# A recurrence whose dense small products are cut apart by large ones, with two additions moved from VectorE to GpSimd

## The reference

```python
q, k, v = x @ Wq, x @ Wk, x @ Wv          # 16 heads of 16
g = sigmoid(x @ Wf + bf)
def step(state, inp):                     # 128 tokens, one after the other
    qt, kt, vt, gt = inp
    state = state * gt[..., None] + vt[..., None] * kt[..., None, :]
    return state, einsum('bhij,bhj->bhi', state, qt)
```

## Time and profile before

| | us |
|---|---|
| median of 3 runs (2298.08 to 2299.51) | 2299.24 |
| the profiled execution: its own time | 2293.58 |
| its span, first to last instruction | 2291.9 |
| TensorE matmul busy | 2122.2 (93%) |
| TensorE weight load busy | 1440.3 (63%) |
| VectorE busy | 1663.3 (73%) |
| ScalarE busy | 1145.6 (50%) |
| GpSimd busy | 311.0 (14%) |

### The profile page before, as it was taken

One profiled execution on the slowest core, in us unless ns is written; L12 is line 12 of the kernel. 1 busy time (PEld: TensorE's weight loads), 2 busy tenths in 40 slices (PEclk: granted clock), 3 DMA queues, 4 the chain that ended last, 5 costly groups with the idle time before them and its releaser, 6 DMA issues. The chain is left out here.

```text
span 2291.9 us, 74706 instructions
## 1 busy us (share of the span) xinstructions
PE 2122.2 (93%) x30263; PEld 1440.3 (63%) x30263; DVE 1663.3 (73%) x3010; ACT 1145.6 (50%) x1887; POOL 311.0 (14%) x282
## 2 busy tenths in 40 slices
PE   6989998989989869999999999999899999999698
PEld 4666666666666657777777777776444444444487
DVE  7777776777777757677776767775555558989897
ACT  3444443444444436766667676665211118855365
POOL 5000000000000011111111111111000005445221
PEclk9999999999999979999999999999899999999899
DMA  3010010010000010101101010100000004459674
GB/s 107 21 30 22 25 27 21 23 29 21 26 26 21 21 47 30 42 27 34 35 27 41 27 41 27 41 27 1 1 0 0 0 1 192 192 211 424 233 269 163
DMA packets 78311, 146.48 MB, mean 64 GB/s; under 512 B 10035, under 2 KB 63542, under 8 KB 78134
## 3 DMA queue, kind: packets, MB, share of 16 engines
q1 hardware_dynamic: 78134, 143.70, 17.9%
HBM read 82.84 MB, written 60.82 MB: 63 GB/s over the span
## 5 line engine op out<-in xcount | busy, mean ns | idle before, releaser
L1281 PE MATMUL ff_bank<-ff_xq,w_uh 128*128 (+1 forms) x1536 | 457.8, 380 | 2.8 <-ACT ff_whole L1390 2.8
L1281 PE MATMUL ff_bank<-ff_xq,w_ul 128*128 (+1 forms) x768 | 291.5, 380 | 0.0
L1281 PEld LDWEIGHTS ff_bank<-ff_xq,w_uh 128*128 128x128 f16 x1536 | 149.9, 98 | 181.3 <-issue 4.1
L1595 DVE TENSOR_REDUCE ff_top<-ff_bank 128x512 f32 (+1 forms) x192 | 132.7, 691 | 116.7 <-PE ff_bank L1281 116.7
L465 ACT ACTIVATE x<-rec_e 128x512 f32<-128x512 f32 x192 | 112.0, 596 | 176.9 <-PE rec_e L348 176.9
L1390 ACT ACTIVATE ff_whole<-ff_bank,ff_coef 128x512 int16<-128x512 f32 x192 | 124.5, 682 | 103.5 <-PE ff_bank L1281 46.4
L1062 DVE TENSOR_REDUCE mneg<-att_s 128x4 f32<-128x512 f32 x256 | 158.9, 683 | 21.1 <-PE att_s L819 20.3
L600 DVE TENSOR_TENSOR rec_tmp<-rec_x,x 32x256 f32<-32x256 f32 (+1 forms) x192 | 80.8, 421 | 126.9 <-PE rec_x L385 62.1
L564 DVE TENSOR_TENSOR x<-rec_x,rec_until 128x512 f32<-128x512 f32 x256 | 158.4, 679 | 12.8 <-PE rec_x L332 12.0
L360 PE MATMUL rec_x<-x 32*32 32x64 f32 x8192 | 147.9, 218 | 21.3 <-issue 12.0
L360 PEld LDWEIGHTS rec_x<-x 32*32 32x32 f32 x8192 | 124.6, 106 | 59.3 <-issue 58.8
(11 more groups left out here) (236 smaller groups left out, 4406.9 us busy)
## 6 DMA issues: line engine op xcount, KB each, us to landing
gate_scratch<-ff_out SPq DMA_DIRECT2D x28, 768.0 KB, 3.5
ff_in<-gate_scratch SPq DMA_DIRECT2D x28, 768.0 KB, 11.0
product_scratch<-ff_out SPq DMA_DIRECT2D x28, 768.0 KB, 9.7
ff_out<-product_scratch SPq DMA_DIRECT2D x28, 768.0 KB, 5.9
att_x<-in_x SPq DMA_DIRECT2D x32, 256.0 KB, 2.7
att_ctx<-in_ctx SPq DMA_DIRECT2D x32, 256.0 KB, 2.9
att_o<-rec_scratch SPq DMA_DIRECT2D x32, 256.0 KB, 3.7
out<-s_out SPq DMA_DIRECT2D x16, 512.0 KB, 3.3
```

What stands on the lines that cost most here:

```text
L1281: m = T.matmul(bank_[:], weights(wp, kc, a, c), tile[:, xp, kc], start=(i == 0), stop=(i == len(terms) - 1))
L1595: V.tensor_reduce(top[:, k, bass.ds(n, 1)], banks[k % 6][:], AX.X, ALU.max, apply_absolute_value=True).then_inc(q1["maxed"], 1)
```

## The change

- **Exponents.** Five sums instead of seven (NE). One matmul result now gives several exponentials: `USES` lists, for each sum, which are taken, `DONE` how many are ready after it. ScalarE takes ten exponentials as before, eight of them with a per-lane bias (`hidden`) that hides the lanes for which they do not hold; before it was four of ten.
- **TensorE's order.** q goes between S0 and S1 in place of vg1. Q is cut in two halves of 32 products with vg0 of the next pair between them. The turn goes between e and I3. vg1 of the next pair comes last in the step. The order is: S0, q, S1, k, I0, k, I1, e, I2, e, turn, I3, e, H, Q first half, vg0, Q second half, e, e, vg1.
- **VectorE.** `floor` comes ahead of the scores, both `scores_out` follow each other, `weighted` part 0 moves to the step of its own pair, between `half_out` and `quarter_out`. L578 (nh) goes to ScalarE. L621 and L623 go to GpSimd (`gather`).
- **GpSimd.** `gather` for each pair; the eight weight-rounding instructions are put one by one behind the first eight gathers.
- The constants are smaller by one mask for each sequence.

```diff
-    NE = 3 + NR
-    EXPS = NR + NE - 1
+    NE = 5
+    EXPS = 2 * NR + 2
+    USES = (((0, 0), (0, 2), (1, 0), (1, 2)), ((0, 1), (1, 1)), ((0, 3), (1, 3)), ((0, NR),), ((0, NR + 1),))
+    DONE = (4, 6, 8, 9, 10)
...
+                def gather(n, s, before):
+                    out = o[:, s].rearrange("p (h i) -> p h i", i=HD)
+                    pool.wait_ge(stored[s], DMAS * (before + 1))
+                    pool.wait_ge(q["added"], 2 * n + 1)
+                    G.tensor_tensor(out, tmp[:, :, 0], tmp[:, :, 1], ALU.add).then_inc(q["added"], 1)
+                    pool.wait_ge(q["added"], 2 * n + 2)
+                    G.tensor_tensor(out, out, tmp[:, :, 2], ALU.add).then_inc(q["out_ready"], 1)
+
+                def levelled(n, flat, r, s, turn_):
+                    if n:
+                        c.wait()
+                    if turn_ in (0, 3):
+                        x = s if turn_ else r
+                        c.did(G.tensor_tensor(blocks_of(flat), blocks_of(flat), spread(x, flat), ALU.mult))
+                    else:
+                        c.did(G.tensor_scalar(flat, flat, 1.0, MAGIC if turn_ == 1 else -MAGIC, ALU.mult, ALU.add))
+
+                for n in range(8):
+                    gather(n, n % 2, n // 2)
+                    levelled(n, *((flat_u, ru, su), (flat_d, rd, sd))[n // 4], n % 4)
+                with pool.Fori(0, (NP - 8) // 2) as j:
+                    for u in range(2):
+                        gather(2 * j + 8 + u, u, j + 4)
...
-                def across_quarter(n):
-                    pe.wait_ge(q["o_taken"], TAKES * n + TAKES + 2)
-                    pe.sem_inc(q["seen"], 1)
-                    for hd in range(H):
+                def across_quarter(n, part):
+                    if part == 0:
+                        pe.wait_ge(q["o_taken"], TAKES * n + TAKES + 2)
+                        pe.sem_inc(q["seen"], 1)
+                    for hd in range(part * HH, (part + 1) * HH):
                         for b in range(2):
                             at = slice(b * D + hd * HD, b * D + (hd + 1) * HD)
                             for chunk in (0, 2):
                                 src, dst = rows(place(b, chunk)), rows(place(b, chunk + 1))
                                 m = T.matmul(X[1][dst, at], mt[src, b, hd, dst], wa[src, 0, at], start=True, stop=True)
-                    m.then_inc(q["o_made"], 1)
+                    if part == 1:
+                        m.then_inc(q["o_made"], 1)
...
                 def products(p, n, s, so, front, back):
                     if back:
                         scores(n, so, 0)
                     if front:
-                        value_gate(p, 1)
+                        across(p, 0, F[1], 0, 0, q["q_made"])
+                        across(p, 0, F[1], 0, 1, q["q_made"])
                     if back:
                         scores(n, so, 1)
                     if front:
-                        across(p, 0, F[1], 0, 0, q["q_made"])
-                        across(p, 0, F[1], 0, 1, q["q_made"])
                         across(p, 1, F[0], 1, 0, q["k_made"])
 
                 def pieces(p, s, before, front, back, more):
                     n, so = p - 1, 1 - s
-                    for i in range(8):
-                        if back:
-                            if i < 4:
-                                inside(n, so, i)
-                            elif i == 4:
-                                across_half(n)
-                            elif i == 5:
-                                across_quarter(n)
-                        if front and i == 0:
-                            across(p, 1, F[0], 1, 1, q["k_made"])
-                        if more and i == 4:
-                            turn(p + 1, so, before + s)
-                        if more and i == 7:
-                            value_gate(p + 1, 0)
-                        if front and i >= 1:
-                            exponents(p, s, i - 1)
+                    if back:
+                        inside(n, so, 0)
+                    if front:
+                        across(p, 1, F[0], 1, 1, q["k_made"])
+                    if back:
+                        inside(n, so, 1)
+                    if front:
+                        exponents(p, s, 0)
+                    if back:
+                        inside(n, so, 2)
+                    if front:
+                        exponents(p, s, 1)
+                    if more:
+                        turn(p + 1, so, before + s)
+                    if back:
+                        inside(n, so, 3)
+                    if front:
+                        exponents(p, s, 2)
+                    if back:
+                        across_half(n)
+                        across_quarter(n, 0)
+                    if more:
+                        value_gate(p + 1, 0)
+                    if back:
+                        across_quarter(n, 1)
+                    if front:
+                        exponents(p, s, 3)
+                        exponents(p, s, 4)
+                    if more:
+                        value_gate(p + 1, 1)
...
+                    act.wait_ge(q["lg_ready"], p + 1)
+                    A.activation(nh[:], nl[:], ACT.Copy).then_inc(q["h_ready"], 1)
...
-                    for k in range(NE - 1):
+                    for k in range(NE):
                         act.wait_ge(q["e_made"], NE * p + k + 1)
-                        A.activation(e[:, s, k], E[(s + k) % 2][:], ACT.Exp).then_inc(q["e_ready"], 1)
-                        if k == 2 and not (isinstance(p, int) and p == NP - 1):
+                        for asks, r in USES[k]:
+                            out = um[:, s, r] if asks else e[:, s, r]
+                            A.activation(out, E[(s + k) % 2][:], ACT.Exp, bias=hidden[:, asks, r:r + 1] if r < NR else 0.0,
+                                         scale=-1.0 if asks else 1.0).then_inc(q["e_ready"], 1)
+                        if k == 1 and not (isinstance(p, int) and p == NP - 1):
                             turned(p + 1)
-                    act.wait_ge(q["e_made"], NE * p + NE)
-                    for r in range(NR):
-                        A.activation(um[:, s, r], E[s][:], ACT.Exp, bias=hidden[:, r:r + 1]).then_inc(q["e_ready"], 1)
...
-                    V.tensor_copy(nh[:], nl[:]).then_inc(q["n_ready"], 1)
-                    dve.wait_ge(q["n_ready"], 2 * p + 1)
                     V.tensor_tensor(nlo[:], nl[:], nh[:], ALU.subtract).then_inc(q["n_ready"], 1)
...
-                def total(n, s, before):
+                def total(n):
                     dve.wait_ge(q["o_taken"], TAKES + TAKES * (n + 1))
                     V.tensor_tensor(tmp[:, :, 0:3], tmp[:, :, 0:3], tmp[:, :, 3:6], ALU.add).then_inc(q["added"], 1)
-                    out = o[:, s].rearrange("p (h i) -> p h i", i=HD)
-                    dve.wait_ge(stored[s], DMAS * (before + 1))
-                    dve.wait_ge(q["added"], 2 * n + 1)
-                    V.tensor_tensor(out, tmp[:, :, 0], tmp[:, :, 1], ALU.add).then_inc(q["added"], 1)
-                    dve.wait_ge(q["added"], 2 * n + 2)
-                    V.tensor_tensor(out, out, tmp[:, :, 2], ALU.add).then_inc(q["out_ready"], 1)
-
                 def step(p, s, before, front, back):
                     n, so = p - 1, 1 - s
+                    if front:
+                        floor(p, 0)
+                        floor(p, 1)
                     if back:
                         scores_out(n, 0)
-                    if front:
-                        floor(p, 0)
-                        floor(p, 1)
-                    if not back:
+                        scores_out(n, 1)
+                    else:
                         sums()
-                    if back:
-                        weighted(n, so, 0)
-                        scores_out(n, 1)
                     if front:
                         split(p)
-                    if not back:
-                        weigh()
                     if back:
                         weighted(n, so, 1)
-                    if back:
                         for k in range(4):
                             inside_out(n, so, k)
                         half_out(n, so)
+                    else:
+                        weigh()
+                    if front:
+                        weighted(p, s, 0)
+                    if back:
                         quarter_out(n, so)
-                        total(n, so, before - so)
+                        total(n)
```

74 lines of the change are left out of this document (35 added, 39 removed).

## The result

The changed kernel takes **2274.56 us** (median of 6 runs, 2270.05 to 2282.8), the kernel before 2296.51 (6 runs, 2292.92 to 2299.51). The ratio is 0.9918, 95% interval 0.9901 to 0.9935: 0.8%, which is 19 us by the ratio and 22 by the two medians, where 41 to 42 us were forecast. The sign and the range of the prediction hold, its size does not. The profiled execution took 2270.66 us (span 2268.9).

What follows compares the result with a forecast made beforehand. TensorE's chain of pieces, with stalls and clock losses, was taken to bound the recurrence. 29 x (0.5 + 0.5 + 0.2) = 35, plus 5 + 1, gave 41 to 42 us gained: 2257 us, range 2236 to 2281.

Steps and rivals of the forecast that it cites:

- What bounds the kernel: Recurrence steps: TensorE's pieces nearly end to end, one real wait at S1, plus lower clock and stalls for instructions.
- undisturbed step: A recurrence step without stalls or clock loss: 22.5 us before, 22.0 after, so 0.5 us less.
- Query wait: TensorE after S0: a new wait of 0.5 us for ScalarE's copy of the value out of F[1].
- S1 wait: TensorE ahead of S1: a wait of 0.3 us for VectorE's scores_out.
- the load lands in time: Next pair's load on SyncE: lands about T + 13.1, turn due at 14.1, T being VectorE's start on Q output.
- Stalls for instructions: TensorE waiting for its own instructions among fast small products: 0.5 us a step less, between 0.3 and 0.8.
- The clock: TensorE's loss at 1.2 GHz in stretches of small products: halved, 0.2 us a step gained, ends 0 and 0.4.
- rival (c): Waits at the query and S1 drop TensorE's clock each step, 1.8 us instead of 0.4: 2299 us, chance 0.06.
- Once only: First steps, where GpSimd's weight rounding holds up VectorE: 8.5 us lost before, 5 us gained by the change.
- The tail: Last step: one weighted part 0 in its way lost, 1.2 us of slower gather gained, 1 us gained.
- Rival (a): Stalls and clock stay, depending on instruction count and chance, not order: about 2274 us, chance 0.22.

Runs made afterwards that it cites:

- e3_mid: Changed kernel with the fourth sum of exponents moved from behind Q to between H and the first half of Q: 2265.58 us.
- before_hq: Kernel before, reordered so that H and the whole Q follow each other (turn ahead of I3, a sum of exponents behind Q): 2319.44 us.
- e3_load: Changed kernel with the fourth sum of exponents between H and the first half of Q, and each load issued ahead of the store: 2260.11 us.
- load_first: Changed kernel with SyncE issuing the load of pair m+2 ahead of the store it would otherwise stand behind: 2275.92 us.
- turn_mid: Changed kernel with the turn moved from between e and I3 to between H and the first half of Q: 2274.9 us.
- late_total: e3_load with VectorE's total moved behind the first four scores_out of the next step, so floor follows the Q output: 2248.86 us.
- dve_adds: Changed kernel with its last two additions back on VectorE behind total, so GpSimd only rounds the weights: 2305.59 us.
- no_round: Kernel before with GpSimd's eight weight-rounding instructions cut to one column each, so its output differs: 2283.93 us.

## Why the prediction was right and wrong

**What bounds the kernel** was read right: TensorE's chain of pieces, its stalls and its clock. The walk through an undisturbed step came out at 21.8 where 22.0 stood. Query wait 0.65 (0.5 forecast), S1 wait 0.31 (0.3), no gap between H and Q (0 taken of 0 to 0.33), GpSimd 1.28 a piece (the row said 1277 ns), `weighted` part 0 ends before Q does, and the load lands in time in 24 of 29 steps. This term is about -0.65 a step, -0.5 was forecast.

**Stalls for instructions.** Idle time marked issue and the restart of the loop body were 1.28 us a step before and are 0.66: -0.62, where 0.5 was taken of 0.3 to 0.8. They went from the second half of Q as expected, but for one of 0.35 us and one of 1.87 in the last step, which has no vg0 between the halves. The reading behind it, that small products side by side outrun their instructions, can be settled from the trace, which holds the transfers of instructions by themselves. In the 29 steps of the kernel before (packets, MB, share of the DMA engines' time):

```profile
q8 instruction: 129, 2.11, 1.3%
```

All 28 stalls of more than 0.3 us before and all 17 after end 1.2 to 1.8 us after such a transfer, which is true of some 10% of the moments of these steps. In `e3_mid` the idle time marked issue alone is 0.11 us a step, in the changed kernel 0.45. The rule of the Trainium skill (Runtime: NRT & Kernel Launch, Instruction fetch mechanics), that crossing a block is mostly hidden, was set aside in the prediction; the two kernels differ by 0.62 x 29 = 18 us in such idle time, so it was right to set it aside here.

**The clock is the step that failed.** "The longest stretch with only small products of 16 columns and little between (H, turn, e, Q: 4.4 us) becomes H and half a Q, 2.6 us. I halve the loss: 0.2 a step, ends 0 and 0.4." Measured: 96 us at 1.2 GHz instead of 30 in the profiled steps, and a mean clock of the runs of 0.959 instead of 0.972, which is some 60 us more of the span at half speed. At 0.31 to 0.53 us each that is, as an estimate, 19 to 32 us lost, some 25, where 6 were to be gained. The error was to measure the stretch from its first small product to its last and to count the turn and the sum in it as nothing. They are what held it. H, turn and e, Q are 2.0 and 1.2 us of products of 16 columns with large ones between; H and half of Q are 2.6 us without. `before_hq` shows it on the old kernel (30 to 96 us at 1.2 GHz by order alone), `e3_load` against `load_first` on the new one (92 to 51), and `turn_mid` that the turn there does little. The rival (c) had the effect, at 1.8 us in each step where it came to some 0.9, but by another cause: the waits at the query and S1. `late_total` without the query's wait speaks against that cause at 1 us; at 2 us, in `dve_adds`, falls stand behind the wait. By its own terms (c) is 2305 us, 0.4 x 29 above 2299 less 6; the 2299 in the prediction takes the 6 off twice. The prediction also counts six steps with a fall before; there are seven. The chance of a dearer clock of 0.06 was too small, and the term's upper end 0 ("no worse than now") had no row behind it.

The Trainium skill (TensorE: Matmul & The Clock Gate, A second HAM failure mode: psum-queue depth-cycling) names brief idle times between groups of matmuls as what makes the clock swing. The falls of `dve_adds` at 3.1 to 3.9 us fit this; the fall at 596.3 does not, since TensorE's busy share is 1.00 in each window of 1 us from 588 on.

**Once only.** 11.8 us ahead of the third S0, 5 forecast. Two steps of that term were off. The loss before is 11.5 (`no_round`), not 8.5: the clock was subtracted from it, and the two falls in the earlier trace rows (0.95 and 0.94) are not in the changed kernel's first steps. That they are not is in part luck: `load_first`, the same kernel there but for its load, has 6.8 us at 1.2 GHz ahead of its third S0 and reaches it at 79.33. And of the 1.6 and 1.9 put against it only 0.53, a wait for nlo, is seen in the first two steps, which took 21.88 and 22.19; about 1 us more may lie ahead of the first S0, which comes 3.0 us later, 1.9 of them for vg1. The pairing of the engines itself was read right.

**The tail.** 1 us gain forecast, 2.2 lost. From the last S0 to the end of Q it is 20.02 us where it was 18.83, and 16.6 us of it stand at 1.2 GHz where it was 8.6. The other microsecond was not followed up.

**The sum.** 19 (undisturbed step), 18 (stalls and restart), 11.5 (first steps), -25 (clock), -2 (turns that wait for their load, 0.07 x 29), -1 (tail beside the clock) are 20.5 us; 19 to 22 were measured. Forecast were 14.5, 14.5, 5, 6, 0 and 1. With 19 to 32 for the clock the sum is 13 to 26, so it fits but does not prove the split. With the clock as it was, the time would have been about 2250, by the same estimate.

**Luck.** The time inside the stated range owes something to it: the stalls and the first steps gave more than forecast and hid part of the clock's loss. Rival (a) named about 2274, almost the measured time, but not its reason: the stalls did not stay, they halved, and the clock did not stay, it got worse.

## What to carry to other kernels

A stretch of small matmuls is not only a stretch of low use: products of 16 columns side by side, without any idle time, can lose TensorE's clock for the large products behind them. When pieces are put in another order, look at which large products separate the small ones, and move existing ones between them before adding any. And where one cause is priced from rows of the old order, let its range reach past "no worse than now", as the new order has no row yet.
